# Second layer's attention on one Trainium2 core: score banks from two to three, head-output banks from two to one

## The reference

```python
Q = (query @ Wq.T + bq).reshape(B, S, H, Hd).transpose(0, 2, 1, 3)   # query = layernorm(x)
K = (key @ Wk.T + bk).reshape(B, S, H, Hd).transpose(0, 2, 1, 3)     # key, value = context
V = (value @ Wv.T + bv).reshape(B, S, H, Hd).transpose(0, 2, 1, 3)
attn = softmax(einsum('bhqd,bhkd->bhqk', Q, K) * scale)
out = einsum('bhqk,bhkd->bhqd', attn, V).transpose(0, 2, 1, 3).reshape(B, S, D)
x = x + tanh(g_xattn[1]) * (out @ Wo.T + bo)
```

## Time and profile before

| | us |
|---|---|
| median of three runs | 2641.68 |
| lowest and highest run | 2639.06, 2643.43 |
| profiled execution, device time | 2637.51 |
| its span from the first to the last instruction | 2635.7 |

### The profile page before, as it was taken

The page is one execution under the profiler, slowest core; times in us unless marked ns, Lnnn a source line. Parts: engine busy times, 40 slices in busy tenths (PEclk is TensorE's granted clock), DMA queues, the critical chain, the costliest instruction groups (busy, mean ns, idle before and its releaser), DMA issues.

```text
span 2635.7 us, 48196 instructions
## 1 busy us (share of the span) xinstructions
PE 2329.9 (88%) x16128; PEld 1936.4 (73%) x16128; DVE 1499.8 (57%) x3906; ACT 1266.7 (48%) x3969; POOL 1022.9 (39%) x907
## 2 busy tenths in 40 slices
PE   5888889888888888988777999999999999999998
PEld 4677777777777777776555877887777778777777
DVE  3467677667667667667676344544444454444441
ACT  5655565555566555565324244443334443333441
POOL 1355554655564555554462133322123322222320
PEclk8989999999999999998788999999999999999999
DMA  4000000000000000001002000000000000000000
GB/s 146 14 6 18 13 10 10 16 16 16 12 16 4 16 16 16 12 8 45 27 13 93 16 13 16 16 16 16 16 4 12 16 16 16 16 4 12 16 9 9
DMA packets 26000, 51.66 MB, mean 20 GB/s; under 512 B 6160, under 2 KB 7312, under 8 KB 24784
## 3 DMA queue, kind: packets, MB, share of 16 engines
q1 hardware_dynamic: 25936, 50.84, 5.9%
HBM read 42.44 MB, written 8.39 MB: 19 GB/s over the span
## 4 chain that ended last, share of the span: by engine, by line
PE 55%; DVE 15%; ACT 12%; issue 7%; DVEq 4%; POOL 4%; POOLq 2%; DMA 0%; ACTq 0%
PE l_ffn L1705 13%; POOL l_prod L384 4%; PE l_attn L160 3%; PE l_ffn L160 3%; PE l_attn L162 3%; PE l_attn L161 3%; DVEq L734 3%; PE l_ffn L161 3%; PE l_ffn L162 3%; PE l_attn L1668 3%; PE l_side L160 3%; ACT l_probs L1369 2%; PE l_attn L1693 2%; PE l_attn L979 2%; PE l_heads L1679 2%
## 5 line engine op out<-in xcount | busy, mean ns | idle before, releaser
L1253 POOL TENSOR_SCALAR l_probs<-l_probs,l_rinv 128x256 f32<-128x256 f32 x512 | 238.9, 481 | 574.6 <-DVE l_rinv L1482 574.5
L1369 ACT ACTIVATE l_probs<-l_score,l_negmax 128x256 f32<-128x256 f32 x512 | 238.4, 472 | 311.6 <-DVE l_negmax L1477 311.5
L384 POOL TENSOR_TENSOR l_prod<-l_att,l_kv 128x2048 f32<-128x2048 f32 x64 | 290.3, 4570 | 179.6 <-DVE l_att L671 176.0
L370 POOL TENSOR_TENSOR l_prod<-l_q,l_kv 128x2048 f32<-128x2048 f32 x64 | 291.8, 4569 | 148.6 <-DVE l_att L654 84.4
L1705 PE MATMUL l_ffn<-l_w,l_hid 128*128 128x256 f32 x1536 | 346.8, 381 | 1.0 <-ACT l_hid L1337 1.0
L1705 PEld LDWEIGHTS l_ffn<-l_w,l_hid 128*128 128x128 f32 x1536 | 287.7, 190 | 50.0 <-issue 13.1
L1489 DVE COPY l_probsT<-l_attn 128x512 f32<-128x512 f32 x256 | 175.6, 686 | 165.9 <-PE l_attn L1668 165.7
L744 DVE CUSTOM_DVE_ANT_0 l_probs<-l_score,l_mbias 128x256 f32<-128x256 f32 (+1 forms) x512 | 161.4, 353 | 145.8 <-PE l_score L946 96.7
L1477 DVE TENSOR_REDUCE l_negmax<-l_score 128x2 f32<-128x512 f32 x256 | 175.2, 684 | 59.9 <-PE l_score L1656 59.1
L677 DVE TENSOR_REDUCE l_h<-l_prod 128x128 f32<-128x2048 f32 x64 | 146.3, 2286 | 101.1 <-POOL l_prod L384 100.8
L467 ACT ACTIVATE l_probs<-l_probs,l_negmax 128x256 f32<-128x256 f32 x256 | 130.8, 511 | 116.6 <-DVE l_negmax L744 115.3
(11 more groups left out here) (266 smaller groups left out, 7551.6 us busy)
## 6 DMA issues: line engine op xcount, KB each, us to landing
l_ctxin<-in_ctx SPq DMA_DIRECT2D x32, 256.0 KB, 3.0
l_xin<-in_x SPq DMA_DIRECT2D x16, 256.0 KB, 2.7
l_x<-in_x SPq DMA_DIRECT2D x16, 256.0 KB, 2.6
x<-l_acc SPq DMA_DIRECT2D x16, 256.0 KB, 2.0
l_xin<-x SPq DMA_DIRECT2D x16, 256.0 KB, 3.2
l_x<-x SPq DMA_DIRECT2D x16, 256.0 KB, 2.7
out<-l_x SPq DMA_DIRECT2D x16, 256.0 KB, 2.0
l_hid<-in_w SPq DMA_DIRECT2D x2, 1536.0 KB, 8.9
```

The lines of the kernel that those rows point to most:

```text
L370: nc.gpsimd.tensor_tensor(prod[:, u].rearrange("p (h g d) -> p h g d", h=half, g=H), q4[:, u * half:(u + 1) * half].unsqueeze(2).to_broadc ...
L384: nc.gpsimd.tensor_tensor(prod[:, u].rearrange("p (h d g) -> p h d g", h=half, d=HD), a4.unsqueeze(2).to_broadcast([P, half, HD, H]), v4.u ...
L1253: last = nc.gpsimd.tensor_scalar(probs[:, j % 4, t * S:(t + 1) * S], probs[:, j % 4, t * S:(t + 1) * S], rinv[:, j, t:t + 1], 1.0, ALU.mul ...
L1369: last = nc.scalar.activation(probs[:, s % 4, t * S:(t + 1) * S], ps[:, t * S:(t + 1) * S], ACT.Exp, bias=negmax[:, s, t:t + 1], accum_out ...
```

## The change

The scores get three banks instead of two. Their list grows by two idle turns, so that 18 uses make six turns of three banks, and TensorE passes the two idle turns before `attn_out`. The outputs of the heads get one bank instead of two, so that heads 8 to 15 write the bank that heads 0 to 7 had. The number of PSUM banks stays at eight. No arithmetic is changed.

```diff
-    score = Banks(nc, left, both, "l1_score", [f"s{j}" for j in range(H)])
-    heads = Banks(nc, left, both, "l1_heads", ["o0", "o1"])
+    score = Banks(nc, left, both, "l1_score", [f"s{j}" for j in range(H)] + ["idle0", "idle1"], 3)
+    heads = Banks(nc, left, both, "l1_heads", ["o0", "o1"], 1)
@@ tensor, body
             yield STEPS
             if a is not None:
+                score.skip(pe, "idle0", a)
+                score.skip(pe, "idle1", a)
                 attn_out(a)
```

## The result

The changed kernel takes 2622.97 us, the median of six runs (2614.45 to 2626.89); the kernel before, measured beside it, took 2642.55 (2639.06 to 2645.37). The ratio is 0.9925 with a 95% interval of 0.9912 to 0.9938, so 19.6 us were saved where 9.9 were forecast. In a later session the same kernel took 2624.67 against 2640.49, ratio 0.9933 (0.9920 to 0.9946), 15.8 us less. The profiled execution took 2621.21 us, 16.3 less than that of before.

What follows compares the result with a forecast made beforehand. TensorE was taken as the bound, with only its waits, 4.2 us a batch, to save. 14 x (0.70 - 0.03) = 9.4 plus 0.5 gave 9.9 us: 2641.7 - 9.9 = 2631.8, range 2627 to 2640.

Steps and rivals of the forecast that it cites:

- Step 6: Scores of heads 6 and 7: a third bank ends their wait for head 5's exponentials, 0.70 us a batch gained.
- twice in each of the 14 batches: Steady batches: scores wait for ScalarE's exponentials only at steps 6 (0.63 us) and 14 (0.71 us), 18.7 us together.
- Step 13: Value products of heads 8 and 9: with one bank they wait for ScalarE's copy, starting 0.82 us later.
- Step 14: Scores of heads 14 and 15: the added wait replaces the one for head 13's exponentials; 0.03 us a batch lost.
- The idle turns: Before the output projection: two added waits and four increments are covered by TensorE's 0.76 us idle; cost 0, 0.05 allowed.
- The number of batches: Third to sixteenth batch, the steady state: 14 x (0.70 - 0.03) = 9.4 us saved.
- The first two batches: Beside the first layer's end: 0 from the first batch, 0.5 us from the second, bounds -1 and +1.5.
- slower, by the clock: Rival: a TensorE gap of about 1.35 us at step 13 makes the granted clock fall; 2649 us, chance 0.07.
- both waits go: Rival: head copy out in time, so step 14 gains its 0.81 us too; 21.6 us saved, 2620.1, chance 0.05.
- The range: Whole kernel: 2627 to 2640 us for 8 in 10; the forecast's own case 2628 to 2636, 0.60 to 0.75 a batch.

Runs made afterwards that it cites:

- the wait put back: Changed kernel, TensorE again waiting at step 6 for head 5's exponentials: batch 77.20 us, median 2629.80 us, ratio to the kernel before 0.9962.
- the one bank alone: Kernel before with one bank instead of two for the heads' outputs, still two score banks: 2637.45 us, ratio 0.9998.
- the run with five: Changed kernel with five idle turns a batch in place of two: 2619.0 us, ratio to the kernel before 0.9937.
- the run with the waits in batch 1: Changed kernel with the old score waits put back in the second batch alone: first to second output projection 102.89 us against 102.48.
- before once more: The kernel before, unchanged, run for a second trace: 2644.03 us.
- early copy in before: Kernel before with ScalarE's copy of heads 0 to 7 moved ahead of head 12's exponentials: 2632.42 us, ratio 0.9980.

## Why the prediction was wrong

The sign, the mechanism and the terms of steps 6, 13 and 14 held; the sum was half of what came, since two waits were not in it.

- **Step 6, forecast 0.70.** Right: 0.70 by the comparison, 0.70 by the wait put back.
- **Exponentials are waited for "twice in each of the 14 batches".** This is the step that failed: the gain of the third bank was put at nothing for every step but 6 and 14. The waits were counted in the table of waits, and that lists only idle time that the product's modelled end leaves visible. At steps 2 and 4, ahead of step 6, two more waits of the same kind stood, worth 0.18 and 0.10 us by the comparison of traces (0.19 and 0.03 came back when they were put in again). The rule that the prediction itself applied to step 6 (a pair takes the banks of heads s-2 and s-1) held for every even step and had to be tried at each. Over fourteen batches 0.28 is 3.9 us; with them the forecast would have been 2627.9, so the rest of the miss has other sources, below. Between step 6 and step 13 there was indeed no other wait: 0.98 us were gained at step 6 and 0.99 at step 12.
- **Step 13, forecast a wait of 1.35 and a start 0.82 later.** Measured 1.28 and 0.76. The release took 0.05 us (0.63 less the copy's 0.58), where 0.11 was taken from the output projection.
- **Step 14, forecast -0.03 net.** Measured +0.02: the copy's quicker release. With the -0.76 and +0.78 of the table the exchange is even, as said; the one bank alone costs nothing. That it is even is a coincidence of two durations, which the prediction had computed from the rows.
- **The idle turns, forecast 0.** Right, by the run with five. The output projection even waits 0.71 in place of 0.76, and starts 0.05 behind the copy's end in place of 0.11. The run with one bank alone has the same (the distance is 60.78 from 60.82 in the second trace of before), so this comes from the heads' banks and not from the turns. It is the last 0.05 of the batch.
- **The number of batches.** 14 x 0.67 = 9.4 was forecast; the third to sixteenth batch gave 1.06 + 12 x 1.04 + 0.94 = 14.5. Of the 5.1 us between, 3.9 are steps 2 and 4 and the rest the hundredths at steps 13, 14 and the output projection.
- **The first two batches, forecast 0.5 within -1 and +1.5.** 1.75 in the first pair of traces and 2.69 in the second, of which the run with the waits in batch 1 supports 0.4. The rest isn't shown to be the score banks': this distance went from 101.83 to 106.67 in the ten traces of kernels with three banks, with the clock's course beside it. Both pairs lie above the bounds.
- **What is left of 19.6.** 14.5 of the steady batches and 0.4 of the second make 14.9, and this much is shown. A fall of the clock of 1.58 us was in two of four traces with two score banks (before, before once more, one bank for the heads, early copy in before) and in none of the ten with three. For the remaining three to four no run shows a cause. The later session gave 15.8, and the interval 0.9912 to 0.9938 reaches down to 16.4, so they can be the scatter of the runs.
- **The rival "slower, by the clock".** It didn't come: in the steady part of the second layer the granted clock stayed at 2.4 GHz in all ten traces of kernels with three banks, nine of which have the gap of 1.28 us in each batch. The prediction compared this gap with one of 2.49 us, but the two falls in the kernel before came behind idle times of 0.53, 0.71 and 0.51 us, so the length of one gap was no guide. The Trainium skill (TensorE: Matmul & The Clock Gate, A second HAM failure mode: psum-queue depth-cycling) tells of a kernel whose short idle times between groups, as it cycled through PSUM banks, made the clock swing. No trace with three banks in rotation shows it here. That three banks prevent the falls isn't shown either: the traces of one bank for the heads alone and of the early copy in the kernel before, both with two score banks, have none in 28 batches.
- **The rival "both waits go".** The measured time lies near its 2620.1, but by chance: its mechanism didn't occur. The copy was not out in time, the value products waited 1.28 us for it, and a batch is 76.50 and not 76.1.
- **The range** was too narrow below: its bound of 0.75 a batch rested on the table's two waits, where 1.04 was measured.

## What to carry over

Where two engines take turns over banks, write down for every step which earlier use frees its bank and when that use ends, and compare it with the start of the waiting instruction; a start that comes later than the flow behind the product ahead of it, and a short time (0.05 to 0.15 us here) behind the releaser's end, is a wait, whatever the table of idle times lists. A missing bank is cheap to give up where its wait falls in front of one that remains or replaces one that goes, and then the work that releases it is worth moving forward: the copy ahead of head 12's exponentials was worth another 0.76 us a batch in the kernel after, and 0.03 in the kernel before.

## What was unexpected of the hardware

**A release of 0.05 or 0.14 us.** The time from the end of ScalarE's exponentials to TensorE's product was 0.14 to 0.15 at steps 2, 4, 6 and 14 of the kernels with two score banks, where the late semaphore was waited for last, and 0.05 where it was waited for first of three (steps 2 and 6), though step 4 answered in 0.06 with the wait last. The last head copy released TensorE in 0.05 with one bank and 0.11 with two. That order matters is shown at step 2 alone, where both orders were run; what causes it isn't shown.

**A VectorE instruction of 0.75 us that takes 3.1 or 8.4.** In the first batch of the second layer line 1471 lies beside GpSimd's products of the first layer. The trace of before, then the second trace of after, VectorE and GpSimd each:

```profile
1367.89 3.08 DVE L1471 SCALAR_TENSOR_TENSOR l_q<-l_qhi,l_again,l_qfull 128x512 fp32r<-128x512 f32 x1
1365.83 4.59 POOL L384 TENSOR_TENSOR l_prod<-l_att,l_kv 128x2048 f32<-128x2048 f32 x1
...
1367.14 8.39 DVE L1471 SCALAR_TENSOR_TENSOR l_q<-l_qhi,l_again,l_qfull 128x512 fp32r<-128x512 f32 x1
1365.10 4.54 POOL L384 TENSOR_TENSOR l_prod<-l_att,l_kv 128x2048 f32<-128x2048 f32 x1
1370.51 4.47 POOL L384 TENSOR_TENSOR l_prod<-l_att,l_kv 128x2048 f32<-128x2048 f32 x1
```

In the first trace it ends 0.55 us behind the end of the GpSimd product that had begun before it (1370.42 to 1370.97). In the second it stays through the end of that product (1369.64), through two short GpSimd instructions and through the next product, and ends 0.55 us behind that one (1374.98 to 1375.53). TensorE then waits 6.7 us for it. The Trainium skill (SBUF — State Buffer, Who interferes with whom) says that a VectorE instruction with two inputs in SBUF contends with a GpSimd instruction that reads SBUF, because its second input comes through a read interface that both share. Both rows agree with that; why the second one isn't served between the two products, no run shows. That makes a part of the runs' scatter. In six traces (among them the first ones of before and of after) the instruction took 2.2 to 3.1 us, and the first output projection came at 1377.8 to 1380.0; in the eight others it took 7.6 to 8.4, and the projection came at 1380.5 to 1385.7.
